# Moving a convolution, three transposes and a row-maximum split to other steps of a hand-written order (attention followed by a Mamba-2 layer, one core)

## What is computed

```python
# layer 0
q, k = wq @ xf + bq, wk @ xf + bk             # 32 rows each
attn = softmax(q.T @ k)                       # 4096 x 4096 per image
x = gamma * (v @ attn.T) + x
# layer 1, tokens u (b, 4096, 256)
u = layernorm(x) * norm_g + norm_b
z, xBC, dt = split(u @ in_w.T)                # 256, 512, 4 columns
xBC = silu(depthwise_conv(xBC, 4 taps) + conv_b)
y = scan_over_tokens(xs, B, C, softplus(dt + dt_bias), A) + Dp * xs
y = rmsnorm(y * silu(z)) * rms_w
out = y @ out_w.T
x = x + out * sigmoid(mlp(mean(out)))
```

## Time and profile before

| | |
|---|---|
| median of 3 runs | 3152.42 us (3150.59 to 3152.76) |
| the profiled execution | 3150.87 us |
| its span, first to last instruction | 3148.7 us |
| mean granted TensorE clock | 0.983 |
| TensorE busy with matmuls | 2980.0 us (95%) |
| VectorE, ScalarE, GpSimdE busy | 2032.0, 1930.0, 2009.9 us |

### The profile page before, as it was taken

One profiled execution on the slowest core, in us unless ns is written; L12 is line 12 of the kernel. 1 busy time (PEld: TensorE's weight loads), 2 busy tenths in 40 slices (PEclk: granted clock), 3 DMA queues, 4 the chain that ended last, 5 costly groups with the idle time before them and its releaser, 6 DMA issues. The chain is left out here.

```text
span 3148.7 us, 63156 instructions
## 1 busy us (share of the span) xinstructions
PE 2980.0 (95%) x21208; PEld 2322.5 (74%) x21208; DVE 2032.0 (65%) x3417; ACT 1930.0 (61%) x3742; POOL 2009.9 (64%) x3087
## 2 busy tenths in 40 slices
PE   6899999999999999999999999999999999999984
PEld 3767777777777777777777777777777777777762
DVE  5556666666666676676676666676666667666654
ACT  2565666666656566666665666666666666666652
POOL 2446666667756576666676656666676667777753
PEclk9999999999999999999999999999999999999986
DMA  3111111111311121222221222122221111212121
GB/s 123 49 37 46 44 51 58 31 54 49 103 63 65 58 71 58 91 77 74 82 77 38 72 76 72 62 76 69 65 89 36 43 49 55 69 50 69 42 95 67
DMA packets 101970, 200.99 MB, mean 64 GB/s; under 512 B 18480, under 2 KB 41392, under 8 KB 97264
## 3 DMA queue, kind: packets, MB, share of 16 engines
q1 hardware_dynamic: 98192, 195.08, 18.6%
q10 hardware_dynamic: 3456, 1.86, 0.2%
HBM read 131.21 MB, written 64.75 MB: 62 GB/s over the span
## 5 line engine op out<-in xcount | busy, mean ns | idle before, releaser
L723 POOL TENSOR_TENSOR p_lo<-p,p_hi 128x512 f16<-128x512 f32 x1024 | 1221.9, 1201 | 845.6 <-ACT p_hi L886 711.9
L879 ACT ACTIVATE p<-p_et 128x512 f32<-128x512 f32 x1024 | 612.2, 598 | 637.4 <-PE p_et L1138 598.0
L1156 PE MATMUL acc<-v_hi,p_hi 128*128 128x257 f16 x4096 | 954.3, 273 | 4.0 <-DVE work L1464 3.8
L1158 PE MATMUL acc<-v_lo,p_hi 128*128 128x256 f16 x4096 | 951.8, 272 | 0.0
L1420 DVE TENSOR_REDUCE maxes<-p_mx 128x1 f32<-128x1024 f32 x508 | 620.1, 1221 | 489.1 <-PE p_mx L1117 488.7
L886 ACT ACTIVATE p_hi<-p 128x512 f16<-128x512 f32 x1024 | 643.5, 629 | 10.0
L1164 PE MATMUL acc<-v_hi,p_lo 128*128 128x257 f16 x4096 | 622.8, 274 | 15.1 <-POOL p_lo L723 15.1
L1156 PEld LDWEIGHTS acc<-v_hi,p_hi 128*128 128x128 f16 x4096 | 399.3, 97 | 125.0 <-issue 54.8
L1158 PEld LDWEIGHTS acc<-v_lo,p_hi 128*128 128x128 f16 x4096 | 400.6, 98 | 117.8 <-issue 49.9
L1164 PEld LDWEIGHTS acc<-v_hi,p_lo 128*128 128x128 f16 x4096 | 399.9, 98 | 68.0 <-POOL p_lo L723 15.9
L1138 PE MATMUL p_et<-qs,kst 98*128 98x256 f16 x2048 | 393.3, 273 | 11.6 <-ACT p L879 11.1
(11 more groups left out here) (213 smaller groups left out, 4164.2 us busy)
## 6 DMA issues: line engine op xcount, KB each, us to landing
work<-rows_d SPq DMA_DIRECT2D x32, 1024.0 KB, 5.2
xin<-in_x_dram SPq DMA_DIRECT2D x48, 512.0 KB, 4.7
xr<-in_x_dram SPq DMA_DIRECT2D x32, 512.0 KB, 3.8
x_d<-x1c SPq DMA_DIRECT2D x31, 512.0 KB, 2.9
og_d<-og SPq DMA_DIRECT2D x29, 512.0 KB, 2.7
mix_x<-x_d SPq DMA_DIRECT2D x25, 512.0 KB, 4.7
mix_o<-og_d SPq DMA_DIRECT2D x24, 512.0 KB, 5.5
out_dram<-mix_o SPq DMA_DIRECT2D x24, 512.0 KB, 2.8
```

What stands on the lines that cost most here:

```text
L723: e.tensor_tensor(p_lo[:, n % RING, :], p32[:, n % P32S, :], p_hi[:, n % RING, :], ALU.subtract).then_inc(lo_pool, 1)
L879: e.activation(p32[:, n % P32S, :], p_et[:, :], ACT.Exp).then_inc(exp_done, 1)
L1156: e.matmul(acc[:, t, 0:C + 1], p_hi[:, r, at:at + P], v_hi[:, 2 * k + kk, 0:C + 1], start=(k == 0 and kk == 0), stop=False)
L1158: e.matmul(acc[:, t, 0:C], p_hi[:, r, at:at + P], v_lo[:, 2 * k + kk, :], start=False, stop=False, skip_group_check=True)
```

## The change

Convolution `m` starts one step later in every group. The first of the four transposes into `xsB` goes from step 25 to 26, the first scaling of y (`K_YN`) from 27 to 26, and the transposes of the second half of the residual (`K_XT`) from step 30 to 19. `load_xr` on SyncE follows them, from step 31 to 20; tanh, `silu` and the copy of the halo follow the convolution. Stage A's dt (`K_DT`) and z (`K_Z`) keep their steps. In VectorE's step `max_parts` stands ahead of `query_rows`, stage B and stage A instead of behind them; it stays in steps 6 and 22 (8 in the first half).

```diff
-K_XBC = (11, 16, 21, 26)
+K_XBC = (12, 17, 22, 27)
 K_Z = (22, 24)
-K_XSB = (25, 27, 28, 29)
+K_XSB = (26, 27, 28, 29)
...
-K_XT = (13, 30)
+K_XT = (13, 19)
 K_XB = 4
 K_RMS = 22
-K_YN = (27, 28)
+K_YN = (26, 28)
...
                     h = n // STEPS + 1
+                    if K % STEPS == (K_PARTS if n >= STEPS else K_PARTS_FIRST) and n // STEPS + 1 < NHALF:
+                        max_parts(n // STEPS + 1)
                     if h < NHALF and K % STEPS == (K_QR if n >= STEPS else K_QR_FIRST):
                         query_rows(h)
...
                 if s < G:
-                    if K % STEPS == (K_PARTS if n >= STEPS else K_PARTS_FIRST) and n // STEPS + 1 < NHALF:
-                        max_parts(n // STEPS + 1)
                     if K == K_BN:
                         bn(0)
```

## The result

The changed kernel takes 3198.92 us (3195.33 to 3201.97, four runs) against 3152.35 us (3150.59 to 3152.76, four runs): a ratio of 1.0148, 95% interval 1.0131 to 1.0166. It is 46.6 us slower; the forecast was 54, and its range of 3174 to 3246 holds the time.

What follows compares the result with a forecast made beforehand. TensorE, busy 95% of the span, was taken to bound the kernel; 44 + 13 - 10 + 5 + 1 + 1 = +54 us on 3150.87, with the runs' median 1.55 higher, gave 3206 us, range 3174 to 3246 (8 in 10).

Steps and rivals of the forecast that it cites:

- The term of step 16: Step 16 without its convolution: `values` waits 1.75 us for `attended` in plain slots; +44 us over all slots.
- the case of a free VectorE: Step 16, only the floor: a wait of 0.95 us (1.27 from slot 0's durations); lower bound +21 us.
- The split ahead of `mt`: Step 6: `max_parts` ahead delays `mt`, 0.5 us in 24 slots and 0.2 in 6; +13 us (0 to 27).
- The transposes: Step 30: the second residual transposes lose their wait of 0.34 us in 29 slots by moving to step 19; -10 us.
- `xsB` and `silu` at 26: Steps 25 and 26: the third convolution's `silu` ends about 0.1 us after `xsB` wants it; +5 us (0 to 12).
- stands ahead of nothing that is late: Step 22: the maxima's split only delays the root's first guess by 1.1 us, its result being needed 4 steps on.
- both terms of step 22: Step 22: the split delays nothing late; z's tanh behind the convolution's copy and tap costs 0.15 in six slots, +1 us.
- VectorE free: Rival: VectorE is free at step 16 and `mt` hidden, so +13 to +23 us, 3165 to 3175; chance 0.18.
- The clock: Rival: the new wait drops the clock to 1.2 GHz in every slot, 46 us on top, 3252; chance 0.10.
- Not slower: Rival: the wait at step 16 doesn't arise; 3134 us, or 3147 with `max_parts`' 13; chance 0.04.
- doubled: Rival: ScalarE or VectorE falls a step behind each slot and `p_et` waits too; above 3250 us; chance 0.06.
- The end: Last three slots, without attention: one chain shifts by a step; +1 us (-3 to +4).

## Why the prediction was right

**The term of step 16** was right in place and mechanism and 3.5 us too large. The wait of 1.70 in plain slots (forecast 1.75), the 0.95 in slots 3, 6, 11, 14 and 22, the reciprocal at 1.05 us into the step, the vanished exp wait and the 31 times are all as stated. Too large were slots 10, 18 and 26 (the wait is 1.71, I had 2.6) and slots 8 and 16 (1.77 for 2.3). That the sum came out so near is in part luck. Over steps 15 to 17 a plain slot loses 1.87 us, not 1.75, and the eighteen together 35, not 31.5; slots 10, 18 and 26 gain 5.4 together where I had a loss of 0.6, partly because in two of them the lower clock level goes with the exp wait. What I called the case of a free VectorE was not one: the 0.95 holds with `silu` ending 0.35 us into the step (0.89 when tried), and with nothing ahead of `attended` the wait is 0.56. So my lower bound of +21 was too high; 31 x 0.56 less the 8.6 of the exp waits gives about +9 (an estimate). The experiments bear the mechanism out from four sides: with the convolution back the wait is gone, other matmuls in the gap take up as much of it as they last, `silu` behind `attended` leaves 0.56, and `silu` at its old place 0.89.

**The split ahead of `mt`** was forecast at 13: 10.7 in steps 7 and 8 of the change, and 11.9 there by itself. It is four instructions (L1425, L1427, L1430, L1432), not the five that I counted ahead of the experiments, and there they keep their length. VectorE's timeline in steps 6 and 7 of the changed kernel, then GpSimdE's:

```profile
2829.90 0.39 DVE L1427 TENSOR_SCALAR mcol<-mcol 128x2 f32<-128x2 f32 x1
2830.36 1.05 DVE L1430 CAST mparts<-mcol 128x2 f16<-128x2 f32 x1
2831.48 0.61 DVE L1432 TENSOR_TENSOR mparts<-mcol,mparts 128x2 f16<-128x2 f32 x1
2832.01 0.68 DVE L1569 TENSOR_TENSOR mt<-pl,lt 128x512 f32<-128x512 f32 x1
```

```profile
2829.65 0.61 POOL L737 TENSOR_TENSOR xd<-xsB,dcol 128x256 f32<-128x256 f32 x1
2830.22 1.15 POOL L723 TENSOR_TENSOR p_lo<-p,p_hi 128x512 f16<-128x512 f32 x1
2831.34 0.73 POOL L813 TENSOR_TENSOR yt<-yt 128x256 f32<-128x256 f32 x1
```

The three take 2.05 us for two elements per partition. In step 22 the same L1427 takes 0.17, where GpSimdE is idle. In steps 6 and 7 each of the three begins while a GpSimdE instruction is running and ends 0.02 to 0.03 us after it: 2830.29 against 2830.26, 2831.41 against 2831.37, 2832.09 against 2832.07. So it is in the whole trace: of the 192 instructions of these three lines 81 take over 0.3 us, and every one of them ends 0.02 to 0.03 us after a GpSimdE instruction that ran beside it; none of the 104 that began with GpSimdE idle is so long. That is the rule which the prediction took from the Trainium skill, SBUF — State Buffer, Who interferes with whom, of a port pair that is held against GpSimdE. The reduce ahead of them (L1425) takes 0.16 every time, beside a running GpSimdE instruction too. No experiment took GpSimdE's work away, so the trace bears the cause out without proving it.

**The transposes** were under-sized: -13.7, and -14.0 alone, for -10. I priced their wait only; step 30 became 27.7 us shorter over the slots, 1.00 in most, and step 19 takes only 14.0 of it, 0.44 each. TensorE's timelines of slot 29 give the parts of the 1.00: the recorded wait of 0.34, 0.49 for the transposes themselves, and 0.17 under the modelled end of the matmuls ahead of them, which the waits don't list (from the start of L1171 to the next matmul 1.38 us, 0.34 of it the wait, and 0.87 in the kernel with the transposes alone). **`xsB` and `silu` at 26** had +6.0 for +5.

**The step of the record that was incomplete** is the sentence that at step 22 the split "stands ahead of nothing that is late", with the parts priced one by one. In the sum it did no harm, because there the split does lie in idle time, so both terms of step 22 come out near 0. But that zero is the work of two parts together. Alone the convolutions cost 104.9 us, the split 16.5 and the transposes -14.0, which makes 107; together they cost 47. In the profiled executions it is 94.1, 17.0 and -13.7 against 47.1. What I took to be free saves some 40 beside the convolutions (28 in the traces), and I had not seen that z's tanh behind the copy and tap makes VectorE wait across the step's end.

**The rivals.** VectorE free (3165 to 3175) is out by the wait of 1.70. With `silu` behind `attended` the time was 3173, inside that range, but by other terms: a wait of 0.56 instead of 0.95, and a split that still cost 11.5 in steps 7 and 8 where the rival had nothing. The clock fell at step 16 in one slot of 31, slot 17, after a wait of 2.07:

```profile
1736.15:1741.23 5.08, 3.01 (x18) 1.91 (x16) 3.32 (x6) 2.33 (x6) 4.13 (x9) 0.82 0.01 2
```

Its steps 16 and 17 took 5.1 and 5.8 us for the 3.84 and 5.02 of a plain slot. In slot 29 both have 1.00, the higher level, and up to the last attention tile the mean is 0.99 in both kernels:

```profile
0.00:3022.50 3022.50, 2907.11 (x20902) 2273.74 (x20903) 1973.61 (x3312) 1891.60 (x3655) 1957.18 (x2983) 0.99 0.19 63
```

```profile
0.00:3065.03 3065.03, 2911.39 (x20907) 2270.89 (x20908) 1988.69 (x3310) 1878.99 (x3655) 1936.88 (x2983) 0.99 0.19 62
```

These are windows of before and after, columns as above. A wait of 1.7 us once a slot was not followed by the lower level in any other slot. Where the wait for exp stays too, as in slots 10, 18 and 26 with the second convolution moved alone, it was: there the rival is right. Not slower and doubled are out by the result. The end is 4.6 us longer for the forecast's 1, just beyond its upper bound of 4, and a kernel that changes nothing there shows 3.9 of the same kind; that it is the clock is read from the windows, and why the clock is granted for longer in one and shorter in the other stays open.

## What to carry over

An accumulator with one buffer needs something between its last use and its next; before moving a block of matmuls away from such a place, look up how long the engine that empties it needs, and what stands ahead of that work in its queue. When several moves are made at once, price each queue as it will stand after all of them: here three parts that cost 107 us one by one cost 47 together. Operations that take turns in one bank have a least distance between them, and moving one without the others breaks it: a distance of four steps instead of five cost 18.4 us at step 21 when the second convolution moved alone.

## What was not expected of the hardware

From the last attention tile to the end, nearly the same work (304 or 308 matmuls) took 122.3 to 131.7 us, at a granted clock of 0.75 to 0.68. Differences of several us between kernels of this family can come from there: 3.9 between two kernels whose orders don't differ in that stretch, 9.4 at most, 0.3% of the time. The stretch up to the last attention tile is the better measure of a change in the slots.
